# Token normalisation moved to GpSimd and rounding of the maxima moved to VectorE in a two-layer gated attention kernel

## The reference, cut to what matters

```python
x = x + tanh(g_xattn[0]) * attention0(layernorm(x), ctx, ctx)     # 16 heads of 16
x = x + tanh(g_ffn[0])   * top2_of_8_experts(layernorm(x))
x = x + tanh(g_xattn[1]) * attention1(layernorm(x), ctx, ctx)
x = x + tanh(g_ffn[1])   * bitlinear_ffn(layernorm(x))            # 256 -> 1024 -> 256
```

## Time and profile before

| | |
|---|---|
| time, median of 3 runs | 761.57 us (759.85 to 763.29) |
| the profiled execution's own time | 759.7 us |
| its span, first to last instruction | 757.9 us |
| mean granted TensorE clock | 0.964 of full |
| busy: PE / DVE / ACT / POOL | 690.8 / 532.2 / 432.1 / 160.3 us |

### The profile page before, as it was taken

How to read it: one execution, slowest core, us unless ns; L and a number is a source line. 1 busy time by engine, 2 the same in 40 slices (tenths; PEclk the granted TensorE clock), 3 DMA queues, 4 the chain that set the end, 5 groups by cost and what they waited for, 6 DMA issues and landing times.

```text
span 757.9 us, 10107 instructions
## 1 busy us (share of the span) xinstructions
PE 690.8 (91%) x3577; PEld 333.1 (44%) x3582; DVE 532.2 (70%) x1137; ACT 432.1 (57%) x568; POOL 160.3 (21%) x279
## 2 busy tenths in 40 slices
PE   5799999999999999989999999998999899988867
PEld 2433433444544545444544445443444344433334
DVE  2777886787887678776787678765886678755243
ACT  3247766773355633575345743568775767568724
POOL 6125343530011220121101220213300311021012
PEclk9769999999999999999999999999999999969999
DMA  7948589214220430224120142116131413000000
GB/s 239 250 123 297 196 250 274 42 44 126 44 47 24 117 94 13 59 44 125 42 44 30 44 127 42 43 74 206 45 70 43 126 28 81 7 2 9 22 1 28
DMA packets 39025, 66.73 MB, mean 88 GB/s; under 512 B 5184, under 2 KB 13888, under 8 KB 38720
## 3 DMA queue, kind: packets, MB, share of 16 engines
q1 hardware_dynamic: 38128, 65.57, 30.5%
q10 hardware_dynamic: 848, 0.53, 0.2%
HBM read 38.29 MB, written 27.26 MB: 86 GB/s over the span
## 4 chain that ended last, share of the span: by engine, by line
PE 61%; DVE 13%; ACT 11%; issue 9%; POOL 5%; DMA 1%; SPq 0%; DVEq 0%; POOLq 0%; ACTq 0%
PE psO L817 11%; PE psS L789 9%; PE psT L803 6%; PE psX L742 6%; PE psX L878 5%; DVE mx L1249 5%; ACT pt L1037 4%; PE psX L879 4%; PE psX L880 4%; PE psX L854 3%; PE psX L762 3%; ACT xn L994 2%; PE psX L930 2%; DVE xs L1380 2%; POOL parts L598 2%
## 5 line engine op out<-in xcount | busy, mean ns | idle before, releaser
L1037 ACT ACTIVATE pt<-psT 128x1024 f32<-128x1024 f32 x256 | 261.6, 1022 | 213.8 <-PE psT L803 211.8
L1249 DVE TENSOR_REDUCE mx<-psS 128x1 f32<-128x512 f32 x512 | 325.5, 681 | 77.2 <-PE psS L789 76.0
L789 PE MATMUL psS<-ks,qs 48*128 48x512 f32 x512 | 152.9, 516 | 9.4 <-DVE mx L1249 8.2
L817 PE MATMUL psO<-pt,vg 128*32 128x512 f32 x1024 | 142.1, 628 | 0.1
L803 PE MATMUL psT<-qs,ks 50*128 50x512 f32 x512 | 118.2, 429 | 7.4 <-ACT pt L1037 6.5
L789 PEld LDWEIGHTS psS<-ks,qs 48*128 48x128 f32 x512 | 60.5, 190 | 129.8 <-issue 76.3
L1380 DVE SCALAR_TENSOR_TENSOR xs<-psX,coef,xs 128x256 f32<-128x256 f32 x128 | 61.9, 483 | 38.9 <-PE psX L880 35.6
L598 POOL TENSOR_TENSOR parts<-qf,parts 128x512 fp32r<-128x512 f32 x30 | 38.3, 1278 | 141.1 <-ACT parts L981 141.1
L803 PEld LDWEIGHTS psT<-qs,ks 50*128 50x128 f32 x512 | 52.3, 190 | 23.8 <-ACT pt L1037 21.1
L878 PE MATMUL psX<-moeh,xh 128*128 128x512 f32 x128 | 57.1, 446 | 1.7 <-DVE xs L1380 1.7
L879 PE MATMUL psX<-moel,xh 128*128 128x512 f32 x128 | 50.7, 396 | 0.0
(11 more groups left out here) (134 smaller groups left out, 759.3 us busy)
## 6 DMA issues: line engine op xcount, KB each, us to landing
ks<-kd SPq DMA_DIRECT2D x64, 192.0 KB, 3.7
qs<-qd SPq DMA_DIRECT2D x64, 192.0 KB, 4.6
kd<-parts SPq DMA_DIRECT2D x16, 512.0 KB, 2.8
qd<-parts SPq DMA_DIRECT2D x16, 512.0 KB, 2.7
kd<-parts SPq DMA_DIRECT2D x16, 256.0 KB, 3.5
qd<-parts SPq DMA_DIRECT2D x16, 256.0 KB, 3.4
ctxb<-in_ctxT SPq DMA_DIRECT2D x7, 512.0 KB, 3.6
xs<-in_x SPq DMA_DIRECT2D x4, 512.0 KB, 6.3
```

Of the source, the lines that this page charges most:

```text
L789: mm(psS[:, i % 3, :], qs[at:at + KR, 2 * g + a, k * P:(k + 1) * P], ks[at:at + KR, 2 * g + a, :], start=True, stop=True).then_inc(pe_s, 1)
L817: i = mm(psO[32 * j:32 * j + 32, :], vg[:, p % 2, k, g * GH + j, :], pt[:, s % RING, j, :], start=k == 0, stop=k == NT - 1, tile_position= ...
L1037: a(pt[:, G % RING, 2 * half:2 * half + 2, :], psT[:], ACT.Exp, scale=SCALE).then_inc(a_exp, 1)
L1249: v.tensor_reduce(mx[:, w // GH % 2, r, col:col + 1], psS[:, i % 3, :], AX.X, ALU.max).then_inc(v_max, 1)
```

## The change

In stages 1 to 7 the normalisation of slot 11 (`LNN` on ScalarE) becomes `LNP` on GpSimd in slot 10, directly behind `LNC`, with a semaphore `p_xn` of its own. The normalisations of layer 1 in slots 13 and 14 of stages 2 to 4, in slots 3 and 4 of stage 5, in stage 0 and at the end stay on ScalarE. `M` moves from GpSimd to VectorE, all 32 times. The second `VV` of stages 1 to 4 moves from slot 10 to slot 11, where it stands behind `M`. `XQ` waits only for whole groups of four `F1` and `LNE` only for whole groups of four normalised tiles; both differ from before only at the end. A semaphore is renamed (`p_ml` to `v_ml`) with its operation left on GpSimd.

```diff
-                put(p, 10, ("VV", (p + 1, 1)))
+                put(p, 11, ("VV", (p + 1, 1)))
...
-        put(p, 11, ("LNN", (int(two), b, 0, NT)))
+        put(p, 10, ("LNP", (int(two), b, 0, NT)))
...
+            def norm_rows(swap, b, t0, t1):
+                i = (n("LNN tiles") + n("LNP tiles")) // NT + 1 + swap
+                if due(p_ln, n("LNC", LN_OPS)):
+                    pool.wait_ge(p_ln, n("LNC", LN_OPS))
...
+                for t in range(t0, t1):
+                    g.tensor_scalar(xn[:, t, :], xs[:, b, t, :], lnw[:, i % 2, 3, t:t + 1], lnw[:, i % 2, 4, t:t + 1],
+                                    ALU.mult, ALU.add).then_inc(p_xn, 1)
...
@@ gpsimd @@
-            def m():
-                g.tensor_copy(p1.bitcast(F32R), top).then_inc(p_m, 1)
-                g.tensor_tensor(p2.bitcast(F32R), top, p1, ALU.subtract).then_inc(p_m, 1)
...
-                if due(p_m, 2 * (i + 1)):
-                    pe.wait_ge(p_m, 2 * (i + 1))
+                if due(v_m, 2 * (i + 1)):
+                    pe.wait_ge(v_m, 2 * (i + 1))
...
-                if due(a_xn, n("LNN tiles")):
-                    dve.wait_ge(a_xn, n("LNN tiles"))
+                if due(a_xn, n("LNN tiles") // NT * NT):
+                    dve.wait_ge(a_xn, n("LNN tiles") // NT * NT)
...
@@ vector @@
+            def m():
...
+                v.tensor_copy(p1.bitcast(F32R), top).then_inc(v_m, 1)
+                if due(v_m, 2 * i + 1):
+                    dve.wait_ge(v_m, 2 * i + 1)
+                v.tensor_tensor(p2.bitcast(F32R), top, p1, ALU.subtract).then_inc(v_m, 1)
...
-                if due(a_f1, n("F1")):
-                    dve.wait_ge(a_f1, n("F1"))
+                if due(a_f1, n("F1") // NT * NT):
+                    dve.wait_ge(a_f1, n("F1") // NT * NT)
```

More of the change, by code:

```diff
@@ L251, in walk @@
         n.n[kind] = n.n.get(kind, 0) + 1
-        if kind in ("LNC", "LND", "LNN", "XQ"):
+        if kind in ("LNC", "LND", "LNN", "LNP", "XQ"):
             tiles = ("LNC" if kind == "LND" else kind) + " tiles"
@@ L391, in build @@
         a_xn = sem("a_xn")
+        p_xn = sem("p_xn")
         a_junk = sem("a_junk")
@@ L614, in ln @@
                     pool.wait_ge(a_xn, n("LNN tiles"))
+                if due(p_xn, n("LNP tiles")):
+                    pool.wait_ge(p_xn, n("LNP tiles"))
                 g.tensor_scalar(ve, var, LN_EPS, None, ALU.add).then_inc(p_ln, 1)
@@ L695, in hquant @@
                 g.tensor_scalar(hh[:, t, :], hh[:, t, :], am[:, 5, t:t + 1], MAGIC, ALU.mult, ALU.add).then_inc(p_hq, 1)
-            walk({"INIT": init, "SPLIT": split, "LNC": ln, "LNE": power, "BIAS": bias, "M": m, "XH": tokens_low, "MH": experts_low,
+            walk({"INIT": init, "SPLIT": split, "LNC": ln, "LNP": norm_rows, "LNE": power, "BIAS": bias, "XH": tokens_low, "MH": experts_low,
                   "XQ": xq, "HQ": hquant}, n)
@@ L771, in xt @@
                     pe.wait_ge(a_xn, n("LNN tiles"))
+                if due(p_xn, n("LNP tiles")):
+                    pe.wait_ge(p_xn, n("LNP tiles"))
                 for t in range(NT):
@@ L983, in ln @@
             def ln(swap, b, t0, t1):
-                i = n("LNN tiles") // NT + 1 + swap
+                i = (n("LNN tiles") + n("LNP tiles")) // NT + 1 + swap
                 if due(p_ln, n("LNC", LN_OPS)):
@@ L1372, in experts @@
                     dve.wait_ge(a_xn, n("LNN tiles"))
+                if due(p_xn, n("LNP tiles")):
+                    dve.wait_ge(p_xn, n("LNP tiles"))
                 if due(v_rt, n("R4", RT_OPS)):
@@ L1426, in f2 @@
                                        in1=xs[:, b, t, :], op0=ALU.mult, op1=ALU.add).then_inc(v_f2, 1)
[L1428 removed]
+            walk({"BOB": scale_bo, "ST": stats, "LNE": variances, "LND": coefficients, "LNV": normalise, "SPLIT": split, "VV": vv, "ABS": abs_sum, "WS": scales, "QUANT": quant, "S": maxima, "M": m,
                   "NT": norm, "OP": op, "R1": router1, "R2": router2, "R3": router3, "R4": router4, "ME": experts, "XQ": xq,
```

44 lines of the change are left out of this document (27 added, 17 removed).

## The result

The changed kernel takes 759.5 us in the median of 20 executions (755.58 to 766.54). The kernel before, run 20 times beside it, takes 765.22 (759.5 to 771.5). The ratio is 0.9943 with a 95% interval of 0.9921 to 0.9965: 0.57% faster, where 756.3 of 761.57, 0.69%, was forecast.

The account below looks back on a forecast made before the run. TensorE's in-order queue was taken to set the pace. End -3.65, maxima -1.5 and normalisation -0.1 sum to -5.25 us: 759.7 to 754.4 for the profiled execution, 756.3 for the median, range 752.0 to 760.5.

Parts of the forecast that it names:

- The end: Serial tail: second scale no longer waits for the first Gelu, -3.5 us, and LNE not for ScalarE, -0.15; together -3.65.
- I count 11 of the 16 exposed waits outside slot 11: Transposes of maxima: rounding on VectorE shortens TensorE's exposed waits by 0.2 us each, 2.2 us, of which 1.5 taken.
- The hold on VectorE: Maxima rounding: a small VectorE operation meeting a GpSimd one is held to about its end, delaying maxima up to 1.2 us.
- Rival (b): Slot 11: VectorE is held for all four normalisations, not one operation; +6.3 us, result 762.7 us; chance 0.14.
- The term of the normalisation and the later `VV`: Stages 1 to 7: normalisation on GpSimd and later value product; -0.4 + 0.4 - 0.1 = -0.1 us.
- I take -0.1 us for each of stages 1 to 4: Slots 10 to 12: the 0.53 us gap closes but comes back in front of `XT`; -0.4 us in all.
- The sign named for this step: Slot 11: the prediction falls if the value product's extraction starts later than 1 us after its products.
- I set these two against each other at -0.1: Stage 5: normalised tokens about 1.28 us later behind a split, while the transpose of maxima wins; net -0.1 us.
- Stage 6's "+0.4": Stage 6: rounding of maxima meets the four GpSimd normalisations with no value product to cover it; +0.4 us.
- (a): Only the end pays, maxima and normalisation swap one wait for another; -3.65 us left, 757.9 us; chance 0.22.
- (c): Half-clock stretches, slots 10 to 15: ending them gives near 751.5 us, chance 0.08; more give 758 to 760, chance 0.05.
- Rival (d): The end: the scale is held by something unseen, so the end wins 1 us instead of 3.65; 759 us; chance 0.08.

Follow-up runs that it names:

- run 20: Not a label: the kernel before was executed 20 times beside the changed kernel; median 765.22 us.
- e7: The changed kernel with the two waits of the end as before; ratio 1.0016 against the kernel before.
- e1: The kernel before with only the two waits of the end relaxed; ratio 0.9932.
- e11: The kernel before with only the two waits of the end relaxed, run once more on another chip; ratio 0.9936.
- e2: The kernel before with only the rounding of the maxima moved from GpSimd to VectorE; ratio 0.9998.
- e4: The changed kernel with the second value product back in slot 10; mean 1 us above the changed kernel's 20 executions, 1.4 below it at equal clock.
- e5: The changed kernel with normalisation back on ScalarE in slot 11 and the second value product back in slot 10; mean 759.1 us.
- e8: The changed kernel itself, run again 12 times beside other versions; its profiled execution took 767.12 us.
- e6: The changed kernel with the normalisation of stages 5 to 7 back on ScalarE in slot 11; 3.5 us below the kernel before at equal clock.
- e9: The changed kernel with the GpSimd normalisation in slot 9 instead of 10, so ahead of a split's subtraction in stage 5; mean 761.0 us.

## Why the prediction was right or wrong

**That the total came near is luck.** The forecast is -3.65 for the end and -1.6 for the body. Measured by ratio, the end alone brings about -5 us and the body alone none (e7: 1.0016). The end won more than its term, and the two terms of the body failed.

**The end: the mechanism was right**, and its 3.65 us are met at equal half-clock time (3.5 and 3.7 in e1 and e11). The term was still mis-sized: from the first Gelu to the second `F1` 4.2 us went instead of 3.5, and it allowed 0.5 us for the clock. With this idle time of TensorE gone, half-clock time is also some 5 to 7 us less per execution (the two sets together 6, +-2), and the end alone brings 0.66% in the mean of the two ratios, about 5 us.

**"I count 11 of the 16 exposed waits outside slot 11, at 0.2 each: 2.2 us, and take 1.5": the waits came as said, the gain in the whole is not shown.** In e2 ten of the 16 lie outside slot 11, not 11 (the slot-11 waits are six, with stage 5), and they shrank by 0.15 to 0.21 us each, 1.8 us together. At full clock 0.8 us of gain are left in stage 0 and 0.8 in stage 5, 1.6 together, near the 1.5. The fitted offset says 0.8 (+-0.4), the ratio 0.9998 with 0.4% either way. Whether the clock took the difference stays open: e2's 2.7 us more at half clock lie within their error.

**The hold on VectorE: right where a split is in flight, too dear in slot 11.** Beside a split the copy took 0.90 us instead of 0.17, and its end came 0.2 us sooner than GpSimd's, at 1.14 instead of 1.34 behind the last maximum. In slot 11 I had `M` held by two normalisations and ending 0.9 us behind the last maximum. It ended 0.61 behind: the copy was not held (0.19), and the subtraction only until the first of the four ended (0.35). Rival (b), a hold for the whole set, is refuted; of the 32 copies more than half took 0.18 us or less. The Trainium skill, "SBUF — State Buffer", section "Who interferes with whom", gives the shared pair to whoever issues first, for the whole instruction; read so, the subtraction waits for one GpSimd operation and not for four, and the trace agrees (153.90 + 0.55 = 154.45, and it ends at 154.48). The same section also counts copies among the operations that can contend for the pair. The copy beside a split agrees (0.90 us). The copy beside a normalisation does not: it takes 0.19 us where the two start within 0.01 us of each other, and 0.22 in e4, where the GpSimd operation had been running for 0.06 us.

**The term of the normalisation and the later `VV`, -0.1 us in all, is the step that failed most.** The changed kernel stands 2.6 us (+-0.5) above e5, which lacks just these two, at equal clock, and 1.5 (+-1.0) in the mean. The prediction looked at the waits on the edited lines and not at the next semaphore behind them: the scores of slot 11 and, in stage 5, the maxima, both waiting for VectorE. Its three parts follow.

**"I take -0.1 us for each of stages 1 to 4": the gap closed as said, the account did not hold.** The 0.53 us gap closed and did not come back in front of `XT`. It came back one step earlier, as a wait of the scores for VectorE. The prediction had this from no row, since it left out the line with 8.2 us. At full clock slots 10 to 13 come out 0.1 us longer (stage 3 of the changed kernel 11.28 us, of the kernel before 11.19); with the half-clock stretch that now falls there they take 1.5 us more in stage 1, and 3.1 in e8, where it is 6.8 us long. The sign named for this step did not come: the extraction of `VV` (L1193 before, L1204 now) starts 0.03 us behind its products.

**"Stage 5 ... I set these two against each other at -0.1": wrong in size.** The transpose of maxima wins 0.8 us, the late tokens cost 1.1, and stage 5 ends 0.45 above the kernel before at full clock (81.26 against 80.81). The price stood in VectorE's queue: `XQ` waits in order, with maxima behind it whose scores are ready, and TensorE waits 1.56 us for the first of them. With stages 6 and 7 the normalisation costs 2.2 us (e6). Stage 6's "+0.4" is open: the transpose waits 0.57 us there in e8, as the 0.53 before, and not at all in the first profile of the changed kernel, where the clock is at half there.

**The price of 480 ns for the normalisation was 554**; the row it came from is of another form: it writes in place and adds a constant, this one has two scalars per token. Four take 2.17 us, more than ScalarE's 2.06. The pair of maxima was priced at 333 ns and took 532 in the mean (325 + 207), and 340 to 360 where nothing held it.

Of the rivals, (a) "only the end pays" is what happened. Of (c), the clock's gain at the end is shown; in the body the stretches moved (19 of 28 against 0 of 28 in slots 10 and 11), and whether they cost more in all is not shown. The profile of the changed kernel has seven half-clock stretches, that of before eight, with the same 54.6 us. Rival (d) is refuted.

What stays open: why the changed kernel's body is 2.3 us dearer than the kernel before at equal clock (e7), when the full-clock stretches that I can compare show about 0.5 in stage 5, 0.1 in slots 10 to 13 of stages 3 and 4 (changed kernel and e6), and a gain of 0.8 in stage 0. One slope for all kernels is a rough tool: a half-clock stretch costs 1.5 us where TensorE is dense, 1.0 in slots 14 and 15 of stage 1, and 0.3 in the tail of e7 (13.8 us from the second `F1` to the last update, 13.5 in the tails without one). The three stretches that `VV` brings into slots 10 and 11 cost 0.2 to 0.6 us more each, so an estimate is 0.6 to 1.8 us of the 2.3. But the profiles of e6 and e9 have them there too, and these two stand 1.7 to 2.2 us lower, so this is not the whole of it.

No version is shown to beat the end alone. e1 and e11 beat the kernel before. The changed kernel they beat by 2.3 us (+-0.4) at equal clock and by 2.7 (+-1.0) in the mean, all sets taken together, though on different chips; the intervals of the ratios overlap. e5 is level with them at equal clock.

## What to carry to other kernels

When a change relaxes a wait in a serial tail and rearranges a full body, run the tail edit alone first: here two relaxed waits gave all of the gain, and the three edits of the body added nothing and, at equal clock, cost 2.3 us. A wait of an in-order engine that is shortened in one place reappears at the next semaphore, so list every wait of the bounding engine around the place, not only those on the edited lines. Before an operation is put on another engine, ask what it stands ahead of there: a late `XQ` held the maxima on VectorE, a normalisation held the maxima on GpSimd. And single profiles do not rank versions that lie this close: the time at half clock differed by 42 us within the 12 executions of e8.

## What the runs showed of the hardware that was not expected

The same program, the changed kernel, was profiled at 755.58 and at 767.12 us, with 54.6 and 81.9 us at half clock; the stretches of these two profiles measure 3.4, 6.8, 13.7 and 20.5 us, and they fall in different slots although stage 1 starts within 0.3 us of the same time in both (from 151.6 and 240.4 in one execution, from 151.1, 164.8 and 253.5 in the other). What decides between the two no run shows. A stretch of 3.4 us costs 1.0 us in slots 14 and 15 of stage 1 (5.40 in e2 against 4.37 us) and 1.5 in slots 10 and 11 (7.39 against 5.87).

A small VectorE operation is held by a GpSimd subtraction with two inputs until that ends (copy of the maxima 0.90 us instead of 0.17; the last operation of `XQ` in e9 1.17 instead of 0.20), while the same copy beside a GpSimd normalisation with one input takes 0.19 to 0.23.

The stretch that the changed kernel had in stage 5 came after TensorE had waited 1.57 us for VectorE (first row, the wait ending at 519.65), the windows view giving the second. In e8 the same wait, 1.56 us, was followed by none, so the wait alone does not decide it:

```profile
519.65 0.49 PE L798 MATMUL psS<-ks,qs 48*128 48x512 f32 x1 [1.57 <-DVE mx L1260]
```

```profile
520.27:527.10 6.83, 6.83 (x25) 3.10 (x24) 2.61 (x5) 3.43 (x4) 0.56 (x2) 0.50 0.96 269
```
